# Second attention layer: scaled output in PSUM, one-column Newton steps with per-row scalars, expert 4's bank cleared ahead of the next maxima

## What is computed

```python
x = rmsnorm(hidden) * ln_w                      # one number per token
q = x @ wq.T ; k, v = ctx @ wk.T, ctx @ wv.T     # 32 heads of 16, 8 kv heads
attn = softmax(q @ k.T / 4)                      # 64 x 64 per sequence and head
hidden = hidden + (attn @ v) @ wo.T
x = layernorm(hidden)                            # one mean, one variance per token
logits = x @ W_gate + b_gate                     # 8 experts, the 2 largest chosen
y = 0.5 * sum over the chosen e of relu(x @ W_e[e] + b_e[e])
hidden = hidden + y
```

## Time and profile before

| | |
|---|---|
| median of three runs | 1801.63 us |
| the profiled execution's own time | 1805.07 us |
| its span, first to last instruction | 1803.3 us |
| TensorE busy | 1700.8 us |
| VectorE busy | 1235.8 us |
| ScalarE busy | 718.5 us |
| GpSimd busy | 484.6 us |
| mean granted clock of TensorE | 0.985 of full speed |

### The profile page before, as it was taken

How to read it: one execution, slowest core, us unless ns; L and a number is a source line. 1 busy time by engine, 2 the same in 40 slices (tenths; PEclk the granted TensorE clock), 3 DMA queues, 4 the chain that set the end, 5 groups by cost and what they waited for, 6 DMA issues and landing times. The chain is left out here.

```text
span 1803.3 us, 31943 instructions
## 1 busy us (share of the span) xinstructions
PE 1700.8 (94%) x12512; PEld 887.9 (49%) x12512; DVE 1235.8 (69%) x2352; ACT 718.5 (40%) x1295; POOL 484.6 (27%) x371
## 2 busy tenths in 40 slices
PE   5889999999999999999999999998899999999998
PEld 2444555555555555554555444444444444444443
DVE  5776666565656556566556577686888888888873
ACT  5443333333333333332334322334444445454442
POOL 0142560803507117057100000000023332232334
PEclk9899999999999999999999999999999999999999
DMA  6122251421403214126220311012534544344340
GB/s 240 36 59 71 57 167 21 133 59 53 136 13 110 79 25 164 25 66 184 68 83 13 135 24 24 1 24 82 173 62 90 85 77 90 71 82 88 67 86 18
DMA packets 231213, 141.52 MB, mean 78 GB/s; under 512 B 215072, under 2 KB 215328, under 8 KB 223136
## 3 DMA queue, kind: packets, MB, share of 16 engines
q1 hardware_dynamic: 163488, 122.77, 25.0%
q10 hardware_dynamic: 67584, 16.79, 5.5%
HBM read 65.60 MB, written 20.97 MB: 48 GB/s over the span
## 5 line engine op out<-in xcount | busy, mean ns | idle before, releaser
L763 PE MATMUL bank<-R 128*128 128x512 f16 (+1 forms) x7152 | 1300.3, 341 | 28.1 <-DVE R L1651 8.8
L763 PEld LDWEIGHTS bank<-R 128*128 128x128 f16 x7152 | 584.7, 98 | 680.9 <-issue 35.6
L1651 DVE SCALAR_TENSOR_TENSOR R<-bank,biases,R 128x512 f16<-128x512 f32 x288 | 204.7, 746 | 224.3 <-ACT R L1229 181.4
L625 POOL TENSOR_TENSOR R<-R 128x512 f32<-128x512 f32 x112 | 144.7, 1292 | 344.1 <-ACT R L1437 342.8
L1229 ACT ACTIVATE R<-bank,biases 128x512 f16<-128x512 f32 x128 | 87.6, 686 | 261.7 <-PE bank L763 252.1
L512 POOL TENSOR_SCALAR R<-R 128x2048 f32<-128x2048 f32 (+1 forms) x20 | 33.0, 1651 | 415.8 <-PE bank L763 351.5
L1437 ACT ACTIVATE R<-R,msk 128x512 f32<-128x512 f32 x128 | 90.5, 718 | 114.3 <-DVE R L2002 114.2
L763 PE MATMUL bank<-CT,R 128*128 128x512 f16 x384 | 95.1, 401 | 23.0 <-DVE CT L1625 11.8
L1663 DVE SCALAR_TENSOR_TENSOR R<-bank,R 64x512 f16<-64x512 f32 x64 | 44.0, 688 | 98.7 <-ACT R L1237 98.3
L1736 DVE SCALAR_TENSOR_TENSOR X<-bank,X 128x512 f32<-128x512 f32 x128 | 86.8, 683 | 32.2 <-PE bank L763 32.1
L1237 ACT ACTIVATE R<-bank 64x512 f16<-64x512 f32 x128 | 75.6, 591 | 54.1 <-PE bank L763 52.9
(11 more groups left out here) (160 smaller groups left out, 1649.2 us busy)
## 6 DMA issues: line engine op xcount, KB each, us to landing
R<-in_wB SPq DMA_DIRECT2D x16, 1024.0 KB, 5.6
R<-in_wX SPq DMA_DIRECT2D x16, 1024.0 KB, 4.8
w_split<-AW SPq DMA_DIRECT2D x16, 1024.0 KB, 4.8
R<-w_split SPq DMA_DIRECT2D x12, 1024.0 KB, 6.7
R<-in_ctxT SPq DMA_DIRECT2D x4, 1024.0 KB, 10.0
X<-in_x SPq DMA_DIRECT2D x4, 1024.0 KB, 13.5
out<-X SPq DMA_DIRECT2D x16, 256.0 KB, 2.0
R<-in_wB SPq DMA_DIRECT2D x7, 512.0 KB, 5.6
```

Source lines behind the costliest of these rows:

```text
L625: g.tensor_tensor(acc, acc, tmp[:, e % 2, :], ALU.add).then_inc(e_acc, 1)
L763: last = pe.matmul(dst, a(sa), b(sb_), start=(k == 0), stop=(k == m - 1))
L1651: v.scalar_tensor_tensor(out=dst, in0=src, scalar=bias, in1=hi, op0=ALU.add, op1=ALU.subtract).then_inc(done, 1)
```

## The change

Three edits, all in the second layer but for the Newton steps, which are shared with the first layer's output normalisation.

1. From tile 2 on, `out_scale` writes its product back over its source in bank 6 (`scaled(n)`), and `out_hi` and `out_lo` read it there. `weigh_v` writes the same bank for the next half, so from tile 2 on it waits for `out_lo` (`b_olo`) of the half before and no longer for `out_scale` (`b_on`).
2. In `newton`, where there is one column (k = 1), the two products by r0 are one TENSOR_SCALAR with r0 as both per-row scalars, and the last product is a TENSOR_SCALAR with one per-row scalar. The semaphore between the two products is counted up by the engine's sequencer instead.
3. Expert 4 of tile n-1 is cleared on DVE right after expert 3, before `less_max(n + 1, 0)`, and `add_and_mean` is gone; on ACT its ReLU stands after expert 3's too, before the exponentials. The same in `step_one`.

```diff
--- before.py
+++ after.py
@@ -207,6 +207,10 @@
 
         def early(n):
             return isinstance(n, int) and n < 2
+
+        def scaled(n):
+
+            return home(n).on if early(n) else banks[home(n).b_pv][:, 0:256]
 
         def s_banks(n, b):
 
@@ -638,13 +642,20 @@
 
             v_, r0, a_, b_, r_ = (s[:, m * k:(m + 1) * k] for m in (0, 2, 3, 4, 5))
             dve.wait_ge(sem_r0, n + 1)
-            nc.vector.tensor_tensor(a_, v_, r0, ALU.mult).then_inc(sem_a, 1)
-            dve.wait_ge(sem_a, n + 1)
-            nc.vector.tensor_tensor(b_, a_, r0, ALU.mult).then_inc(sem_a2, 1)
+            if k == 1:
+                dve.sem_inc(sem_a, 1)
+                nc.vector.tensor_scalar(b_, v_, r0, r0, ALU.mult, ALU.mult).then_inc(sem_a2, 1)
+            else:
+                nc.vector.tensor_tensor(a_, v_, r0, ALU.mult).then_inc(sem_a, 1)
+                dve.wait_ge(sem_a, n + 1)
+                nc.vector.tensor_tensor(b_, a_, r0, ALU.mult).then_inc(sem_a2, 1)
             dve.wait_ge(sem_a2, n + 1)
             nc.vector.tensor_scalar(a_, b_, -0.5, 1.5, ALU.mult, ALU.add).then_inc(sem_b, 1)
             dve.wait_ge(sem_b, n + 1)
-            nc.vector.tensor_tensor(r_, r0, a_, ALU.mult).then_inc(sem_r, 1)
+            if k == 1:
+                nc.vector.tensor_scalar(r_, r0, a_, None, ALU.mult).then_inc(sem_r, 1)
+            else:
+                nc.vector.tensor_tensor(r_, r0, a_, ALU.mult).then_inc(sem_r, 1)
             dve.wait_ge(sem_r, n + 1)
 
         def root(act, s, k, n, sem_arg, sem_ln, sem_r0):
@@ -1047,7 +1058,9 @@
                     pe.wait_ge(b_tev, n * 2 + b + 1)
                 else:
                     pe.wait_ge(pr_in, (n * 2 + b - 3) * 16)
-                if b == 1 or n >= 2:
+                if n >= 2:
+                    pe.wait_ge(b_olo, n * 2 + b)
+                elif b == 1:
                     pe.wait_ge(b_on, n * 2 + b)
                 pl = home(n)
                 for blk in range(16):
@@ -1490,7 +1503,7 @@
 
             def out_hi(n, b):
                 act.wait_ge(b_on, n * 2 + b + 1)
-                sc.activation(home(n).onh[:, b, 0, :], home(n).on, ACT.Copy).then_inc(b_ohi, 1)
+                sc.activation(home(n).onh[:, b, 0, :], scaled(n), ACT.Copy).then_inc(b_ohi, 1)
 
             def turned_o(n):
                 act.wait_ge(a_to, n + 1)
@@ -1503,8 +1516,6 @@
             def norm_hi(n):
 
                 norm_root(act, ffn_stat(n), 0)
-                if n > 0:
-                    expert(n - 1, 4)
                 if n >= 2:
                     act.wait_ge(fn_in, (n - 1) * 16)
                 tile_hi(act, ffn_stat(n), 0, yn, ffn_turn(0) + 1)
@@ -1530,6 +1541,7 @@
                 turned_o(n)
                 tile_hi(act, attn_stat(n + 2), 1, yn, attn_turn(2) + 1)
                 expert(0, 3)
+                expert(0, 4)
                 act.wait_ge(a_y, n + 1)
                 exponentials(2, 0)
 
@@ -1553,6 +1565,7 @@
                     act.wait_ge(an_in, (n - 1) * 16)
                     tile_hi(act, attn_stat(n + 2), 1, yn, 0)
                 expert(n - 1, 3)
+                expert(n - 1, 4)
                 if more:
                     exponentials(n + 1, 0)
 
@@ -2064,13 +2077,13 @@
                 pl = home(n)
                 dve.wait_ge(b_o, n * 2 + b + 1)
                 dve.wait_ge(b_rec, n * 2 + b + 1)
-                v.tensor_tensor(pl.on.rearrange("p (k d) -> p k d", d=16), banks[pl.b_pv][:, 0:256].rearrange("p (k d) -> p k d", d=16),
+                v.tensor_tensor(scaled(n).rearrange("p (k d) -> p k d", d=16), banks[pl.b_pv][:, 0:256].rearrange("p (k d) -> p k d", d=16),
                                 wide(smx[:, 32:48], 16), ALU.mult).then_inc(b_on, 1)
 
             def out_lo(n, b):
                 pl = home(n)
                 dve.wait_ge(b_ohi, n * 2 + b + 1)
-                v.tensor_tensor(pl.onh[:, b, 1, :], pl.on, pl.onh[:, b, 0, :], ALU.subtract).then_inc(b_olo, 1)
+                v.tensor_tensor(pl.onh[:, b, 1, :], scaled(n), pl.onh[:, b, 0, :], ALU.subtract).then_inc(b_olo, 1)
 
             def add_out(n):
                 dve.wait_ge(a_y, n + 1)
@@ -2078,11 +2091,6 @@
                 v.scalar_tensor_tensor(out=xt, in0=banks[home(n).b_y], scalar=UN2, in1=xt, op0=ALU.mult, op1=ALU.add).then_inc(a_add, 1)
                 alone(dve, a_add, n + 1)
                 norm_stats(dve, ffn_stat(n), 0, xt, False)
-
-            def add_and_mean(n):
-
-                add_out(n)
-                expert(n - 1, 4)
 
             def step_one():
                 n = 1
@@ -2114,8 +2122,9 @@
                 norm_apply(dve, attn_stat(n + 2), 1, x_tile(n + 2), yn)
                 tile_lo(dve, attn_stat(n + 2), 1, yn, 0)
                 expert(0, 3)
+                expert(0, 4)
                 less_max(2, 0)
-                add_and_mean(n)
+                add_out(n)
 
             def attn_step(n, odd):
                 more, norm = has(n, -1), has(n, -2)
```

## The result

| | before | after |
|---|---|---|
| median of six runs, us (lowest to highest) | 1802.01 (1801.3 to 1805.49) | 1779.17 (1772.51 to 1782.88) |
| profiled execution, us (span) | 1805.07 (1803.3) | 1777.49 (1775.7) |
| one step, turned output to turned output, median of the ten from tile 3's to tile 13's, us | 32.67 | 30.85 |

The ratio of the medians is 0.9871 (95% interval 0.9854 to 0.9887): 1.3% faster, where 1779 us was forecast.

The account below looks back on a forecast made before the run. TensorE, busy 94% of the span, was taken as the bound, so only its waits could give time. Terms 9.8 + 6.6 + 4.3 + 1.6 = 22.3 off 1801.6 gave 1779 us; 8-in-10 range 1775 to 1790.

Parts of the forecast that it names:

- Scaled output, 11 x 0.89: Turning of the scaled output: `out_lo` falls from 1.37 to about 0.43 us, PE's wait goes, 9.8 us saved.
- The new wait on `b_olo`, 0: PE before second-half `weigh_v`: now waits for first-half `out_lo`, which ends before PE starts there; cost 0.
- Expert 4's place, 12 x 0.55: PE's expert 6 no longer waits for DVE to clear its bank: 0.55 us a step, 6.6 us.
- the projection, 4.3: PE's projection no longer waits for `probs_lo`, with DVE 0.4 us ahead of PE: 4.3 us saved.
- vanishes doubly: Last Newton product's 1.09 us block on DVE goes because expert 4's POOL sum moves ahead and the form has one tensor input.
- the rival of a partial wait: A new DVE wait uses up the 0.4 us before the projection, adding 0.2 to 0.5 a step: 1784 to 1790; chance 0.22.
- Newton forms, nothing by themselves: One-column Newton chain of four on DVE: -0.07 to +0.1 us, where DVE idles anyway, so no gain.
- The DMA wait, 3.4: PE's wait at `weigh_v` for the transposing DMA stays, since gate and chain shift together: 3.4 us shown remain.
- Last tiles, 1.6: PE's 2.01 us DMA wait before the gate in step 14 falls by 1.3, behind step 15 another 0.3.
- The sum: Scaled output 9.8, expert 4 6.6, projection 4.3 and last tiles 1.6 make 22.3 us; chance 0.58.
- The mask meeting POOL, 0.08: Slower rival: mask on DVE meets POOL's last sum into X, up to 2 us x 13 added, 1805 us; chance 0.08.
- the point of decision, 1.3 us: Mask and POOL's last sum meet if the gate comes earlier against POOL by over about 1.3 us.

Follow-up runs that it names:

- after_again: The changed kernel, unaltered, run and profiled again: 1781.37 us, 0.9873 of the kernel before.
- no_newton: The changed kernel with the one-column Newton steps back in their old form: 1777.22 us, 0.9874 of the kernel before.
- psum_only: The kernel before with only the scaled output kept in PSUM: 1793.05 us, 0.9938 of the kernel before.
- newton_only: The kernel before with only the one-column Newton steps in the new form: 1794.14 us, 0.997 of the kernel before.
- long_last_sum: The forced case: changed kernel with one more 512-column POOL sum before its sum into X: 1790.82 us, 0.9964 of the kernel before.
- both_first: Changed kernel with `probs_lo` ahead of `row_sums` on DVE and `out_hi` ahead of expert 2's ReLU on ScalarE: 1774.1 us, 0.9843 of before.

## Why the prediction was right, point by point

**Scaled output, 11 x 0.89.** Right in kind and size: 0.885 alone, 0.90 as the last edit (31.745 without it, 30.845 with it). `out_lo` took 0.425 in all of tiles 2 to 15, and it ends at 1456.11 where PE is free at 1456.36: 0.25 to spare, 0.2 forecast (0.20 to 0.34 in the other steady steps). By the rule of the Trainium skill, "VectorE: DVE Perf Modes", its section on the errata of SBUF sources, it would have grown by 0.06 (estimate from that page); the four `out_lo` of the early tiles, with SBUF sources, took 0.420 in the same run and the 28 with a PSUM source 0.425. No such difference.

**The new wait on `b_olo`, 0.** Right: `out_lo` of the first half ends at 1452.09, PE starts `weigh_v` at 1452.94 and is held by the DMA.

**Expert 4's place, 12 x 0.55, and the projection, 4.3.** Forecast together: 0.55 a step and 4.3 / 12 = 0.36. The order edit, which was to remove both waits, gave 0.905 alone, and 31.42 - 30.845 = 0.575 where the Newton forms had already taken the projection's. So 0.55 holds, and "vanishes doubly" is what the table shows. Two small slips: the trace has 13 such waits of expert 6 and not 12 (2 of the 15 in the earlier trace rows lie in the last tiles), and the 0.43 of the earlier trace rows is the longer of two values that come in turn, though the 4.3 was taken from the total and so has the mean. The step in the middle was worked out badly: `probs_lo` was to be 0.4 us ahead of PE, and is 0.15 in every second step (it ends at 1439.69, PE starts at 1439.84) and 0.35 in the others. It ended on the right side by less than half of what I had, and the rival of a partial wait was nearer than its 0.22 says.

**Newton forms, nothing by themselves.** Right for the changed kernel (0.06 a step, ratios alike), and the price per row was inside its bounds: two per-row scalars took 0.266 us, one 0.214. A chain of three now takes what four had.

**The DMA wait, 3.4.** 4.0 in 12 times, the same as before within 0.6.

**Last tiles, 1.6.** 1.92 + 0.2 = 2.1. The wait before the gate fell by 0.6 only, not by 1.3 (PE before, then after; the twelve matmuls behind it in the second line of each):

```profile
1746.21 0.46 PE L763 MATMUL bank<-g1w,R 128*128 128x8 f16 x12 [2.01 <-DMA R<-R]
1746.52 4.34 PE L763 MATMUL bank<-R 128*128 128x512 f16 x12
```

```profile
1718.80 0.46 PE L774 MATMUL bank<-g1w,R 128*128 128x8 f16 x12 [1.41 <-DMA R<-R]
1719.11 2.75 PE L774 MATMUL bank<-R 128*128 128x512 f16 x12
...
1726.12 2.76 PE L774 MATMUL bank<-R 128*128 128x512 f16 x12 [0.87 <-DVE R L2015]
```

What I had not seen is that the wait of 2.01 also had cost 4.34 - 2.75 = 1.59 behind itself, at half the clock; that fell away, and a new wait for an expert's bank (0.87 at 1726.12) and a longer one for the DMA behind it (0.96 in place of 0.39) took part of it back. So the size came out near the forecast by two terms that it did not have.

**The sum.** 20.7 was forecast for the steps, eleven or twelve times each term. Eleven steps gave 19.32 (19.49 in `after_again`). Of the 2.90 of the step to tile 2 a part is the clock: in the kernel before it stood at 0.72 on the mean from 1305 to 1310 us, behind a wait of 2.54, and in the changed kernel at 1.00 behind the same wait of 2.94. `no_newton`, whose steps are those of the changed kernel, had a fall as long as the kernel before had, and took 37.48 for it against 39.34. So some 1.9 are the change's, an estimate from those two, and the steps gave about 21. The mechanism and the size of the terms were right; that the median came to 0.2 us of the forecast was luck. With six runs over 10 us it isn't itself known to 0.2, the interval of the ratio stands for 20 to 26 us, and the same two kernels on another chip differed by 20.75 (1802.12 and 1781.37) where these medians differ by 22.8.

**The mask meeting POOL, 0.08.** It did not happen: in the step shown the gate is 0.27 ahead of POOL's sum as before (1443.74 and 1444.01; the earlier trace rows: 1455.54 and 1455.81), and in every second step 0.07, later against it by the 0.2 that was forecast. But the point of decision, 1.3 us, was wrong, as the forced case shows.

## What to carry to other kernels

When an engine's rows of one operation come in two lengths, lay the rows of the other engines beside them before rewriting the operation: here a PSUM operand, a scalar in place of a one-column tensor, or shorter work on the other engine each removed the same block. A freed block can move to the next instruction that POOL can block, of the same form (0.80 in `psum_only`) or of another (1.08 in `newton_only`), and two cures of one wait don't add, so run each edit alone and left out alone, and compare the length of a step, which repeats to hundredths of a microsecond where single runs move by several. After a gain look for what is now first with least to spare: the last wait here (0.2 us) was worth having only together with the activation behind it.

## What the runs showed of the hardware

**The clock at a wait.** TensorE's granted clock fell to its lower level (1.2 of 2.4 GHz) at the end of some waits of 2 to 3.1 us or just behind them, and at others of that length it did not. Columns: us, busy time of the engines, granted clock, DMA share, GB/s; the kernel before, at its wait of 3.08 us that ends at 854.08 (first layer), then at the one of 2.01:

```profile
853.00:860.00 7.00, 5.92 (x16) 2.41 (x17) 1.41 (x2) 1.30 (x3) 4.71 (x5) 0.52 0.52 179
```

```profile
1748.00:1751.00 3.00, 3.00 (x19) 1.25 (x18) 2.55 (x9) 2.12 (x4) 1.59 (x2) 0.51 0.13 48
```

In the changed kernel the same first-layer wait was 2.83 and no fall followed: the twelve matmuls there took 2.76 us and not 5.30. With that, 3.2 of the 3.24 us ahead of the first turned output are reached within 7 us (a group starts at 860.48 before, its like at 857.29 after). In `long_last_sum` one step was 34.66 us and not 31.76, with the clock at half for 3.4 us behind a wait of 2.3. What decides whether a fall follows was not tried. The first turned output, ahead of which at most the one-column Newton forms differ, came between 1237.85 and 1247.25 us in the thirteen profiles: 1243.1 to 1247.3 in the six with a fall at 851 to 858 us, 1237.9 to 1242.9 in the seven without one. So the falls go with a good part of the spread between runs; that they are its cause is likely, and not shown.

**What POOL blocks on DVE.** Blocked in this kernel, while POOL adds 512 f32 columns: TENSOR_TENSOR with two SBUF tensors, at 256 columns and at one, a CAST of 8 columns (1.09 for 0.17) and a TENSOR_SCALAR of 8 (in the last tile before, and 1.12 for 0.23 in `long_last_sum`). Not blocked: the same TENSOR_TENSOR with one operand in PSUM, and one-column TENSOR_SCALARs with none, one or two per-row scalars. A TENSOR_SCALAR of 512 columns with per-row scalars is blocked too: 1.08 in `newton_only` above, and 1.20 in `both_first` (12 of 28 at 1.2), where it takes 0.55 in the changed kernel, beside POOL's sum of 1487.08 to 1488.34:

```profile
1487.42 1.20 DVE L744 TENSOR_SCALAR yn<-X,stat 128x512 f32 x1
```

So what the one-column forms escape, a TENSOR_SCALAR of 8 or 512 columns does not: width matters as well as the operands. What it is between 1 and 8 was not tried.
